# Gathering graph features: on-chip fields and indices in place of a staged load per group of edges

## The reference, cut to what matters

```python
# L0: mean of neighbours        m = h[src] * edge_weight;  agg = segment_sum(m, dst)
# L1: stochastic aggregation    m = h[src] * (mu + spread * edge_attr); agg = segment_sum(m, dst)
# L2: GATv2, 5 heads            e = leaky_relu(xl[src] + xr[dst]); softmax over dst; sum of shares * xl[src]
# L3: relational GAT, 4 heads   rows xw[edge_type, src]; q[edge_type, dst] + k[edge_type, src]; softmax; sum
```

## Time and profile before

| | us |
|---|---|
| runs, median (lowest to highest of 3) | 11397.69 (11395.51 to 11404.53) |
| the profiled execution, its time | 11410.16 |
| its span, first to last instruction | 11408.1 |

### The profile page before, as it was taken

How to read it: one execution, slowest core, us unless ns; L and a number is a source line. 1 busy time by engine, 2 the same in 40 slices (tenths; PEclk the granted TensorE clock), 3 DMA queues, 4 the chain that set the end, 5 groups by cost and what they waited for, 6 DMA issues and landing times. The chain is left out here.

```text
span 11408.1 us, 146167 instructions
## 1 busy us (share of the span) xinstructions
PE 6336.2 (56%) x31639; PEld 4385.4 (38%) x31640; DVE 6968.2 (61%) x9723; ACT 1664.8 (15%) x5751; POOL 5957.6 (52%) x6263
## 2 busy tenths in 40 slices
PE   1777777676666764555276455544743332923327
PEld 1555454444444432222166222224732221722226
DVE  6777545577767767777888677778941112711118
ACT  0222344200000001000065100004610000000000
POOL 2777677577767735666200266640007775057760
PEclk8666778666666656666555566665555555855558
DMA  2333444444444426888388388865923333333333
GB/s 66 93 91 92 111 124 126 102 122 120 116 110 122 121 64 209 261 263 263 96 350 333 124 263 262 264 189 216 388 103 87 85 85 67 98 91 85 85 78 105
DMA packets 983109, 1719.05 MB, mean 151 GB/s; under 512 B 527619, under 2 KB 597268, under 8 KB 929127
## 3 DMA queue, kind: packets, MB, share of 16 engines
q1 hardware_dynamic: 577360, 1118.77, 28.7%
q0 software_dynamic: 227424, 434.31, 17.6%
q10 hardware_dynamic: 178256, 165.14, 4.4%
HBM read 1271.04 MB, written 448.16 MB: 151 GB/s over the span
## 5 line engine op out<-in xcount | busy, mean ns | idle before, releaser
L537 POOL DMA_INDIRECT gathered_rows<-node_table,stage x2912 | 2800.0, 962 | 1245.8 <-issue 874.4
L537 POOL DMA_INDIRECT gathered_rows<-xl_table,stage x1664 | 1572.9, 945 | 1916.3 <-DMA stage<-slots 1436.6
L537 POOL DMA_INDIRECT gathered_rows<-rel_table,stage x1664 | 1570.1, 944 | 1908.4 <-DMA stage<-slots 1401.8
L557 PE MATMUL ps_sum<-messages,onehots 128*125 128x65 f32 (+3 forms) x13312 | 2209.2, 339 | 529.2 <-DVE messages L1654 246.3
L557 PEld LDWEIGHTS ps_sum<-messages,onehots 128*125 128x125 f32 x13312 | 2154.3, 254 | 660.8 <-issue 655.3
L680 PE MATMUL ps_G<-table_parts,low_onehots 125*128 125x400 bf16 x4992 | 1551.3, 486 | 818.7 <-DVE low_onehots L691 797.2
L1420 PE MATMUL ps_Z<-xr_parts,onehots_turned 125*128 x4992 | 1293.5, 437 | 1116.1 <-DVE z L1446 1067.3
L698 DVE TENSOR_TENSOR rows_by_feature<-ps_G,high_onehots 128x400 f32<-128x400 f32 x1664 | 944.3, 574 | 1159.0 <-PE ps_G L680 1126.4
L1532 PE MATMUL ps_Q<-query_parts,onehots_turned 125*128 x4992 | 655.3, 205 | 1486.9 <-DMA onehots_turned<-onehots_turned 1484.4
L1420 PEld LDWEIGHTS ps_Z<-xr_parts,onehots_turned 125*128 125x128 bf16 x4992 | 654.4, 131 | 1755.9 <-issue 1350.8
L680 PEld LDWEIGHTS ps_G<-table_parts,low_onehots 125*128 125x128 bf16 x4992 | 587.1, 128 | 1606.0 <-issue 1183.8
(11 more groups left out here) (297 smaller groups left out, 5087.8 us busy)
## 6 DMA issues: line engine op xcount, KB each, us to landing
stash_a<-gathered_rows SPq DMA_DIRECT2D x208, 1300.0 KB
kept_rows<-stash_a SPq DMA_DIRECT2D x208, 1300.0 KB
onehots<-onehots_kept SPq DMA_DIRECT2D x520, 500.0 KB
onehots_turned<-onehots_turned SPq DMA_DIRECT2D x416, 250.0 KB
stash_r<-gathered_rows ACTq DMA_DIRECT2D x208, 272.0 KB
kept_rows<-stash_r SPq DMA_DIRECT2D x208, 272.0 KB
onehots_kept<-onehots ACTq DMA_DIRECT2D x104, 500.0 KB
gathered_rows<-node_table,stage POOLq DMA_INDIRECT x2912
```

The lines of the kernel that those rows point to most:

```text
L537: pool.indirect_dma_start(G[:, HALF * k + q, 0:width], None, table, bass.IndirectOffsetOnAxis(stage[:, k, field, q:q + 1], 0)).then_inc(ga ...
L557: return nc.tensor.matmul(ps_sum[0:BN, bass.ds(at, width)], S[:, j, :], M, start=False, stop=True, skip_group_check=True)
```

## The change

1. **Fields stay on chip.** `rec`, `slots`, `stage` and `staged` go. ScalarE's copies in the set-up now land in tiles that stay in SBUF: `src_all`, `dloc`, and until the end of the segments phase `weight_all`, `low_all`, `high_all`. The field BLOCK goes. The two fields of the relation stages, 896 KB, go to `types_dram` and are read back before R1 in a block of their own.
2. **Indices are copied on chip.** ScalarE copies the eight index columns of a group into `IDX` (`keep_index`), after that slot's gathers of the turn before have landed. In H and W it copies the weights of the group too, into `W`.
3. **GpSimd waits itself** for what frees the slot (sums, adds, stash), then for the index. SP no longer waits for the stash in P, R and H.
4. `pick_rows` reads the high part through a moving slice, with TENSOR_TENSOR in place of TENSOR_SCALAR. `load_low_row` waits for the comparison that last read its slot. Tiles used early are given back (`early.close()`).

```diff
-SRC, SRC_TYPE, BLOCK, DLOC, WEIGHT, SRC_LO, SRC_HI, TYPE = range(8)
+SRC, SRC_TYPE, DLOC, WEIGHT, SRC_LO, SRC_HI, TYPE = range(7)
...
-        slots = nc.dram_tensor("slots", [NG, P, R * HALF], I32, kind="Internal").ap()
+        types_dram = nc.dram_tensor("types", [P, 2, NS], I32, kind="Internal").ap()
...
+        src_all = sb("src_all", [P, NS], I32)
...
+        weight_all = sb("weight_all", [P, NS], F32, early)
+        low_all = sb("low_all", [P, NS], F32, early)
+        high_all = sb("high_all", [P, NS], F32, early)
...
-                    sp.dma_start(slots.rearrange("g p r -> p g r"), rec[:, :, :, :].rearrange("p g a e -> p g (a e)")).then_inc(s_slotD, 16)
+                    sp.dma_start(types_dram, kept).then_inc(s_slotD, 16)
...
-                        if a == DLOC:
-                            nc.scalar.activation(dloc[:, :], ps_turn[:, a % 2, 0:NS], ACT.Copy)
-                        dest = rec[:, :, a, :] if a in (SRC, SRC_TYPE, BLOCK) else rec[:, :, a, :].bitcast(F32)
-                        nc.scalar.activation(dest, ps_turn[:, a % 2, 0:NS].rearrange("p (g e) -> p g e", e=HALF), ACT.Copy).then_inc(s_slotC, 1)
+                        dest = (src_all[:, :], kept[:, 0, :], dloc[:, :], weight_all[:, :], low_all[:, :], high_all[:, :],
+                                kept[:, 1, :].bitcast(F32))[a]
+                        nc.scalar.activation(dest, ps_turn[:, a % 2, 0:NS], ACT.Copy).then_inc(s_slotC, 1)
...
-                    link(v.tensor_copy(fin[:, BLOCK, :, :], be[:, 0, :].unsqueeze(2).to_broadcast([P, NT, C])))
...
-        def stage_group(sp, stage, i, k, others=()):
...
+        def chunks_free(engine, i, k):
+
+            engine.wait_ge(chunk_done.sem, chunk_done.at((i - 1) * U + HALF * (k + 1)))
+
+        def rows_free(pool, i, k):
+
+            chunks_free(pool, i, k)
+            pool.sem_inc(pool_seen, 1)
+            pool.wait_ge(stashed[k].sem, stashed[k].at(16 * i))
+
+        def keep_index(act, IDX, index, i, k):
+
+            nc.scalar.activation(IDX[:, k, :], index[:, bass.ds(i * U + HALF * k, HALF)], ACT.Copy).then_inc(index_kept.sem, 1)
+
+        def gather_loop(pool, G, width, table, IDX, free, count=HALF):
             with pool.Fori(0, TURNS) as i:
                 for k in range(K):
-                    pool.wait_ge(staged[k].sem, staged[k].at(16 * i + 16))
+                    free(pool, i, k)
+                    pool.sem_inc(pool_seen, 1)
+                    pool.wait_ge(index_kept.sem, index_kept.at(K * i + k + 1))
                     pool.sem_inc(pool_seen, 1)
...
         def load_low_row(sp, LR, i, k):
+            sp.wait_ge(low_made.sem, low_made.at(K * (i - 1) + k + 1))
...
-            dve.wait_ge(staged[k].sem, staged[k].at(16 * i + 16))
-            v.tensor_scalar(HI[:, k, :], pos[:, 0:NB], stage_f[:, k, SRC_HI, HALF - 1:HALF], None, ALU.is_equal).then_inc(high_made.sem, 1)
+            chunks_free(dve, i, k)
+            v.tensor_tensor(HI[:, k, :], pos[:, 0:NB], high_all[:, bass.ds(i * U + HALF * k + HALF - 1, 1)].to_broadcast([P, NB]),
+                            ALU.is_equal).then_inc(high_made.sem, 1)
...
 (weighted_sums, ScalarE)
+                        for k in range(K):
+                            keep_index(act, IDX, src_all, 0, k)
...
-                                    act.wait_ge(staged[k].sem, staged[k].at(16 * i + 16))
+                                nc.scalar.activation(W[:, k, :], weight_all[:, bass.ds(i * U + HALF * k, HALF)], ACT.Copy).then_inc(weights_kept.sem, 1)
+                                act.wait_ge(weights_kept.sem, weights_kept.at(n + 1))
                                 act.wait_ge(gathered[k].sem, gathered[k].at(16 * (HALF - 1) * (i + 1)))
...
                                 last.then_inc(msg_made.sem, 1)
+                                keep_index(act, IDX, src_all, i + 1, k)
...
 (weighted_sums, VectorE, with hist)
-                                    dve.wait_ge(staged[k].sem, staged[k].at(16 * i + 16))
+                                    chunks_free(dve, i, k)
+                                    dve.wait_ge(stashed[k].sem, stashed[k].at(16 * i))
...
 (attribute_sums, ScalarE)
-                                act.wait_ge(chunk_done.sem, chunk_done.at((i - 1) * U + HALF * (k + 1)))
+                                act.wait_ge(gathered[k].sem, gathered[k].at(16 * (HALF - 1) * i))
+                                keep_index(act, IDX, src_all, i, k)
+                                chunks_free(act, i, k)
...
 (pair_scores, SP)
                                 sp.wait_ge(z_made.sem, z_made.at(4 * (K * i + k - 1)))
                                 sp.sem_inc(sp_seen, 1)
-                                sp.wait_ge(stashed[slot].sem, stashed[slot].at(16 * ahead))
-                                sp.sem_inc(sp_seen, 1)
-                                stage_next(ahead, slot)
+                                load_turned(sp, ST, ahead, slot)
...
 (pair_scores, GpSimd)
-                        gather_loop(pool, stage, G, GW, xl_table, SRC)
+                        def added_and_stashed(pool, i, k):
+                            pool.wait_ge(z_made.sem, z_made.at(4 * (K * (i - 1) + k + 1)))
+                            pool.sem_inc(pool_seen, 1)
+                            pool.wait_ge(stashed[k].sem, stashed[k].at(16 * i))
+
+                        gather_loop(pool, G, GW, xl_table, IDX, added_and_stashed)
...
 (pair_scores, ScalarE)
+                                if m % 4 == 3:
+                                    act.wait_ge(gathered[m // 4].sem, gathered[m // 4].at(16 * HALF * (i + 1)))
+                                    keep_index(act, IDX, src_all, i + 1, m // 4)
...
 (relation_scores, ScalarE)
                                 stash_group(act, G, FR, stash_r, i, k)
+                                keep_index(act, IDX, src_type, i + 1, k)
...
+        kept_types = sb("kept_types", [P, 2, NS], I32)
+        types_back = sem("types_back")
+        with nc.Block() as block:
+            @block.sync
+            def _(sp):
+                sp.dma_start(kept_types[:, :, :], types_dram).then_inc(types_back, 16)
+                sp.wait_ge(types_back, 16)
```

More of the change, by code:

```diff
@@ L489, in build @@
         coef_made = Counted("coefficients_made")
-        staged = [Counted(f"staged_{k}") for k in range(K)]
         gathered = [Counted(f"gathered_{k}") for k in range(K)]
@@ L716, in weighted_sums @@
             with es:
-                stage = sb("stage", [P, K, R, HALF], I32, es)
-                stage_f = stage[:, :, :, :].bitcast(F32)
+                IDX = sb("index", [P, K, HALF], I32, es)
+                W = sb("weights", [P, K, HALF], F32, es)
                 G = sb("gathered_rows", [P, U, D], F32, es)
@@ L745, in _ @@
                             for k in range(K):
-                                if hist:
-                                    stage_group(sp, stage, i, k, (stashed[k],))
-                                else:
-                                    stage_group(sp, stage, i, k)
+                                if not hist:
+                                    chunks_free(sp, i, k)
                                     load_onehots(sp, S, i, k)
@@ L828, in _ @@
                     def _(pe):
-                        for c in (msg_made, *(() if hist else (turned_copied,)), *stashed, chunk_done, bank_picked):
+                        for c in (msg_made, *(() if hist else (turned_copied,)), *stashed, chunk_done, bank_picked, low_made):
                             nc.tensor.nop().then_inc(c.sem, c.credit)
@@ L872, in _ @@
                                              skip_group_check=True).then_inc(finished, 1)
-                for c in staged:
-                    c.over(16 * TURNS)
                 for c in gathered:
@@ L877, in weighted_sums @@
                 chunk_done.over(NCH)
-                for c in (msg_made, *((onehot_made,) if hist else (narrow_made, turned, turned_copied))):
+                index_kept.over(GROUPS + K)
+                for c in (msg_made, weights_kept, *((onehot_made,) if hist else (narrow_made, turned, turned_copied))):
                     c.over(GROUPS)
@@ L994, in _ @@
                                          skip_group_check=True).then_inc(finished, 1)
-                for c in (*staged, *onehots_in):
+                for c in onehots_in:
                     c.over(16 * TURNS)
@@ L1001, in attribute_sums @@
                 chunk_done.over(NCH)
+                index_kept.over(GROUPS)
                 for c in (msg_made, coef_scaled, coef_made):
@@ L1482, in _ @@
                         turn(TURNS - 1, True)
-                for c in (*staged, *loaded, *stashed):
+                for c in (*loaded, *stashed):
                     c.over(16 * TURNS)
@@ L1537, in _ @@
                     def _(act):
+                        for k in range(K):
+                            keep_index(act, IDX, src_type, 0, k)
                         with act.Fori(0, TURNS) as i:
@@ L1713, in build @@
```

(1 more changed line is left out.)

82 lines of the change are left out of this document (36 added, 46 removed).

## The result

| | before, us | changed, us |
|---|---|---|
| median of 4 runs | 11396.6 | 11132.6 |
| lowest to highest | 11391.8 to 11404.5 | 11125.6 to 11134.4 |
| the profiled execution, its time | 11410.2 | 11125.6 |
| its span | 11408.1 | 11123.7 |

The ratio is 0.9767 with an interval of 0.975 to 0.9783: 264 us less, where 240.5 less (11157 us) was forecast. The measured time lies inside the stated range of 11076 to 11290.

A forecast was written before the change was run, and what follows sets the result against it. The bound was taken to change by stage: GpSimd's gathers, the VectorE-TensorE loop in A, late gathers in P. Terms -254 - 7.5 + 26 + 5 - 16.5 + 6.5 = -240.5 us from 11397.7 gave 11157 us, range 11076 to 11290.

The forecast's parts named there:

- P1 and P2, -254: Pair stages: 1168 and 1166 us fall to GpSimd's floor of 1040 us each once the queued stage load goes.
- GpSimd's added waits, +26: GpSimd's group starts: extra waits cost 0.05 us a group over 520 groups, range 0 to 285 us.
- Rival (d): GpSimd's sequencer at group starts: added waits make the kernel slower from 0.256 us each; 11547 us at 0.4; chance 0.04.
- Set-up, -16.5: Set-up: a write of 896 KB replaces that of `slots` (-13.7 us), and fewer copies save some 2.8 us.
- ScalarE in W, +5: Stage W: ScalarE's added weight and index copies cost 5 us, bounds 0 and 26.
- L693, 0 with 8 kept: VectorE's high-part comparison with two SBUF operands beside gathers: 0 taken, 8 us possible in W.
- Stage starts and the read-back: Index copies replace DMAs at five stage starts (-7.5 us); reading 896 KB back in a new block adds 6.5 us.
- A1 and A2, 0: A stages: the loop of VectorE and TensorE is the bound, so no gain; bounds 0 and -19 us each.
- (a): P stages: DMA engines become the bound and half of P's gain is lost, 11284 us; chance 0.18.
- (b): A1 and A2 gain as well, 19 us each, 11119 us; chance 0.10.
- (c): P stages: GpSimd waits for the stash instead, groups stay at 11.2 us, 11411 us, no change; chance 0.04.

The follow-up runs named there:

- experiment 1: Kernel before, but SP issues stage load and turned one-hots of group n+2 ahead of the stash of group n in P: 11272.3 us, ratio 0.9889.
- experiment 2: Kernel before, but SP issues stage load and turned one-hots of group n+2 ahead of its wait for group n's landing in P: 11147.2 us, ratio 0.9788.
- experiment 6: Kernel before with L693 as TENSOR_TENSOR alone: 11398.0 us (ratio 1.0002); with its old comparison made four times a group: 11406.8 us (1.0006).
- experiment 4: Changed kernel with two, twelve or sixty more already-met waits at every GpSimd group start: 11139.5, 11136.8 and, on a slower chip, 15288.8 us.
- experiment 5: Changed kernel with half of each gathered group (650 KB) written a second time behind the stash in P: 11216.8 us.
- experiment 8: Kernel before with SP's load ahead of the landing and VectorE's low comparison earlier in A: 11095.3 us; changed kernel with that comparison and the read-back moved: 11069.5 us.

## Why the prediction was right, and where it was not

- **P1 and P2, -254:** measured -251.2. The size came from the floor and was right (it was taken from windows rounded up by 1.7 us each, which makes the 3 us too many). The reason given, a small load behind a big write, was half of it. The 22.8 us of the earlier trace rows hold 6.6 us from the last gather's end to the landing, and SP asks for nothing in that time; I took this as given and looked only at what came behind it. Experiments 1 and 2 part the two: of P1's 127 us, 63 came with the queue place and 64 with the landing. The 2.5 us for a load on an empty queue were 3.9 between gathers.
- **GpSimd's added waits, +26:** 0. The mis-sized term, and with it most of the 24 us by which the forecast was too slow. I reasoned from the gap of one wait and bounded by whole gaps. What the runs showed in its place: a wait already met is worked through while earlier gathers run, some 15 us before the gather behind it. The bounds were also counted unevenly: the 285 us hold nine added waits over the eight stages, rival (d) ten, and the prediction's own list gives twelve. Rival (d), 0.256 us a wait from where it decides, was out of reach: twelve more waits changed nothing.
- **Set-up, -16.5:** -20.0. The small write holds the next phase 4.0 us, not 5, which gives 14.7 of them. The write also starts 3.3 us sooner, where 2.8 was forecast for fewer copies (three of 1.07 us by the row that it took are 3.2), and 2.0 lie behind it, between the next phase and H's first gather.
- **ScalarE in W, +5:** +0.5. The copies lie in its waits for gathers, as argued; the 5 us of caution were not needed.
- **L693, 0 with 8 kept:** W's gathers took 690.7 us in all, against 690.2, and with the new form alone 690.2. The Trainium skill, "SBUF — State Buffer", Who interferes with whom, by which W could have lost up to 26 us, is not borne out at this size. In H, however, the 205 gathers beside L553 (1000 elements, two operands) took 1.08 to 1.17 us on average (the slower half had L813's second comparison beside them too), and those beside the table's split up to 2.9 us; beside L813's first comparison, also 1000 elements from two operands but written as bf16, they took 0.944. Two operands alone don't tell which instruction holds a gather up.
- **Stage starts and the read-back:** -6.3 and +5.5 against -7.5 and +6.5. That the first fits is in part luck: only 4.2 of the 6.3 us lie ahead of W, P2 and R2, 2.4 ahead of A1 and 2.4 behind R2's last gather, where nothing was forecast, and the way to P1 grew by 2.5. Moving the read-back beside other work takes 4.7 of the 5.5 back.
- **A1 and A2, 0:** -13.5 in the one profile, but 3.5 us a stage between the means of the runs. Experiment 6 shows that the time of VectorE's comparison doesn't count on the path, experiment 4 added waits for GpSimd and saw 929 to 937. What the few microseconds are is open; they are smaller than the scatter of single profiles.
- **The rivals:** (a) did not come, and experiment 5 says how far off it was: 19% more GB/s cost 28 us a stage. (b) came in sign but not as a gain that stands out of the scatter. (c) and (d) did not come; the wait of (c) shows only under the extra writes of experiment 5.

## What to carry to other kernels

Before you take a transfer away because it is slow, ask when it is asked for. Here a two-line move in the issuing engine's program, the load ahead of the wait for a landing, was worth some 245 of the 264 us; keeping the data on chip was worth the other 20 or so (15 to 24 by the ratios of experiments 2 and 8). And where two engines in a loop both show waits for each other while the third only waits for slots, move the first link of the loop ahead of the work that doesn't need it: that gave 50 to 60 us more.

## What the runs showed of the hardware

- GpSimd's sequencer is far ahead of its gathers: in R1 of the changed kernel it works through a group's met waits, 0.096 us each, 15.1 us before the group's first gather, with up to twelve gathers handed on and not yet begun. It needs 4.1 us for a group whose gathers take 9.98, so 12 waits more cost nothing; with sixty more, on a slower chip, it took 14.8 us a group and set the pace. A wait that is not yet met is dearer: when the load's semaphore came at last, the gather began 0.75 us later. The Trainium skill, "Perfetto Trace Analysis", DMA Instruction — SWDGE (GPSIMD), draws a queue between the sequencer and the cores that work on a gather; this trace agrees.
- A gather's row ends long before its data is there: 0.94 us on the row, and 7.2 us from the end of the last one to SP's wait for the landing being over, while a stash of 1300 KB was under way (experiment 1, also its median over P1; in the kernel before the median is 5.6).
- A DMA share near 0.9 is no bound by itself. Between 0.88 at 288 GB/s and 0.94 at 344 GB/s this kernel moved a fifth more.
